# Causal attention: the probabilities of chunks 0 and 1 turned by the DMA in fp16 pairs, attended as one pair

## The reference, cut to what matters

```
energy = einsum('bhsk,bhtk->bhst', Q, K)          # 16 heads of 32 channels
lengths = sum(energy[:, :, 0, :] != 0, axis=-1)
energy = where(cols >= lengths, -inf, energy)
energy = where(cols[None, :] > cols[:, None], -inf, energy)
score = softmax(energy / sqrt(dk), axis=-1)
out = einsum('bhst,bhtk->bhsk', score, V) * m
x1 = layernorm(x + out)
```

## Time and profile before

| | us |
|---|---|
| median of 3 runs (lowest, highest) | 2641.38 (2639.04, 2642.63) |
| the profiled execution, its own time | 2641.75 |
| its span (first to last instruction) | 2640.0 |

### The profile page before, as it was taken

How to read it: one execution, slowest core, us unless ns; L and a number is a source line. 1 busy time by engine, 2 the same in 40 slices (tenths; PEclk the granted TensorE clock), 3 DMA queues, 4 the chain that set the end, 5 groups by cost and what they waited for, 6 DMA issues and landing times.

```text
span 2640.0 us, 67260 instructions
## 1 busy us (share of the span) xinstructions
PE 2585.4 (98%) x23144; PEld 2230.3 (84%) x23144; DVE 1940.1 (73%) x5443; ACT 1553.5 (59%) x4738; POOL 923.6 (35%) x1102
## 2 busy tenths in 40 slices
PE   6999999999999999999999999999999999999997
PEld 5888888887888888888888888888788888888886
DVE  7888898887433444345388888888788888888877
ACT  6778778785111111111287777777676776767764
POOL 5776677751101010101013333333333434334341
PEclk8999999999999999999999999999999999999999
DMA  6676677674211111203021111112322212222210
GB/s 190 162 189 172 174 171 179 174 181 136 64 48 55 41 51 44 63 32 106 21 82 48 48 48 48 48 48 81 117 73 71 88 64 74 85 65 98 68 48 25
DMA packets 313622, 236.12 MB, mean 89 GB/s; under 512 B 150736, under 2 KB 240848, under 8 KB 312656
## 3 DMA queue, kind: packets, MB, share of 16 engines
q1 hardware_dynamic: 313552, 235.22, 31.3%
HBM read 137.65 MB, written 63.96 MB: 76 GB/s over the span
## 4 chain that ended last, share of the span: by engine, by line
PE 75%; DVE 11%; ACT 8%; issue 5%; DMA 1%; POOL 0%; DVEq 0%; SPq 0%; ACTq 0%; POOLq 0%
PE cross_work L181 16%; PE mlp_f L3282 13%; PE mlp_acc L3300 13%; PE causal_work L181 10%; PE cross_scores L2298 3%; PE cross_scores L2275 2%; PE cross_attended L2328 2%; PE causal_scores L2298 2%; ACT mask_prob L975 2%; PE causal_scores L2275 2%; DVE mask_scores L1560 2%; PE mask_work L181 2%; ACT mask_prob_even L975 2%; PE causal_attended L2328 2%; DVE mask_stats L1473 1%
## 5 line engine op out<-in xcount | busy, mean ns | idle before, releaser
L3075 ACT ACTIVATE mlp_h<-mlp_f,mlp_b1col 128x512 f32<-128x512 f32 x128 | 88.3, 690 | 526.6 <-PE mlp_f L3282 526.6
L3282 PE MATMUL mlp_f<-mlp_xT_hi,mlp_w 128*128 128x512 f32 x1024 | 335.4, 389 | 0.0
L3182 DVE CAST mlp_hT_hi<-mlp_h 128x512 fp32r<-128x512 f32 x128 | 58.3, 455 | 369.8 <-ACT mlp_h L3075 369.6
L3300 PE MATMUL mlp_acc<-mlp_w,mlp_hT_hi 128*128 128x512 f32 x1024 | 315.2, 389 | 0.0
L975 ACT ACTIVATE cross_prob<-cross_scores,cross_low 128x256 f32<-128x256 f32 x512 | 237.5, 490 | 63.4 <-DVE cross_low L1554 63.4
L975 ACT ACTIVATE causal_prob<-causal_scores,causal_low 128x128 f32<-128x128 f32 (+1 forms) x512 | 210.6, 437 | 93.7 <-DVE causal_low L1560 93.6
L3282 PEld LDWEIGHTS mlp_f<-mlp_xT_hi,mlp_w 128*128 128x128 f32 x1024 | 192.1, 188 | 40.6 <-DVE mlp_xT_lo L3168 0.4
L3300 PEld LDWEIGHTS mlp_acc<-mlp_w,mlp_hT_hi 128*128 128x128 f32 x1024 | 192.2, 188 | 39.9
L1560 DVE CUSTOM_DVE_ANT_0 mask_scores<-mask_scores,mask_mask 128x256 f32<-128x256 f32 x512 | 200.5, 459 | 28.7 <-PE mask_scores L2275 24.2
L181 PE MATMUL causal_work<-causal_xT_hi,causal_w 128*128 128x256 f32 x1008 | 217.0, 293 | 0.3 <-DVE causal_qk_parts L1508 0.3
L736 POOL TENSOR_SCALAR causal_q<-all_own_head,causal_qk_parts 128x128 fp32r<-128x128 f32 x128 | 60.7, 486 | 405.9 <-DVE causal_qk_parts L1508 395.6
(11 more groups left out here) (370 smaller groups left out, 8072.4 us busy)
## 6 DMA issues: line engine op xcount, KB each, us to landing
cross_x_in<-after_attention SPq DMA_DIRECT2D x17, 512.0 KB, 4.0
mask_x_in<-in_x SPq DMA_DIRECT2D x16, 512.0 KB, 4.5
mask_c_in<-in_ctx SPq DMA_DIRECT2D x16, 512.0 KB, 4.8
mask_res<-in_x SPq DMA_DIRECT2D x16, 512.0 KB, 3.7
after_attention<-mask_res SPq DMA_DIRECT2D x16, 512.0 KB, 3.3
mlp_x<-after_attention SPq DMA_DIRECT2D x8, 1024.0 KB, 5.5
mlp_stage<-in_L_xattn_fc_w SPq DMA_DIRECT2D x8, 1024.0 KB, 5.7
after_layer<-mlp_y SPq DMA_DIRECT2D x8, 1024.0 KB, 4.4
```

What stands on the lines that cost most here:

```text
L3282: ins = pe.matmul(F1[m % 2][:], W[2 * (m // 4)][:, a, k, m % 4 * P:(m % 4 + 1) * P], xT[p][:, k, :], start=(k == 0 and n == 0), stop=(k == ...
L3300: ins = pe.matmul(ACC[t][:], hT[a][:, m % 2, t * P:(t + 1) * P], W[2 * (m // 4) + 1][:, p, m % 4, :], start=(m == 0 and n == 0), stop=(m = ...
```

## The change

In the turns 1 to 14 of the causal phase, chunks 0 and 1 go the way of the mask phase's even chunks. `exps` of them writes to a new buffer `prob_even` of four heads; ACT's `causal_high` writes their fp16 high halves to `P16` and POOL's `causal_low` the low halves, two heads a step; SP issues two transposing DMAs a chunk (`causal_over`) to `PT16`, which has room for both chunks; `causal_parts` attends both chunks, five products each, directly ahead of `scores(b, 3)`. The eight `turn_probs` and `copy` of these chunks go. V's even parts are split in three. The turn has programs of its own, `causal_loop`, on ACT, DVE, PE and a branch on POOL, and their order differs from `causal_turn` in more than that, as the diff shows. The counts of `copied` follow (`turned_before`); the cross phase waits for the last such attend before it loads over the new buffers. The lift by 10 is added to `low` as in the mask phase.

```diff
--- before.py
+++ after.py
...
@@ -297,6 +300,13 @@
     if causal:
+        low = r("low", [P, 4, TT, 2])
+        at_end = room(REST + 44 * KB, 27 * KB)
+        prob_even = at_end("prob_even", [P, 4, 3 * P])
+        P16 = at_end("prob_parts", [P, 2, 2, 2, 3 * P], F16)
+        PT16 = at_end("probT_parts", [P, 2, 2, 2, 2, 3, P], F16)
+        VP = [at_end(f"v_part{i}", [P, TT, 2, P], BF16) for i in range(3)]
+        V_EVEN = V[:, :, 0:2 * HC].rearrange("p t (g h) d -> p t g (h d)", g=2)
...
@@ -381,21 +391,27 @@
-    def crossed(c):
-        return masked_ctx and c % 2 == 0
+    def crossed(b, c):
+        return masked_ctx and c % 2 == 0 or causal and not isinstance(b, int) and 0 <= c < 2
     def turned_before(b, c):
-        return turned_by_pe(kind) * b + HC * (c // 2 if masked_ctx else c)
+        if masked_ctx:
+            return UNITS // 2 * b + HC * (c // 2)
+        if cross or isinstance(b, int) and b == 0:
+            return UNITS * b + HC * c
+        if not isinstance(b, int) or b < B - 1:
+            return UNITS // 2 * b + UNITS // 2 + HC * (c if c < 0 else max(0, c - 2))
+        return UNITS // 2 * (B - 1) + UNITS // 2 + UNITS * (b - B + 1) + HC * c
     def low_of(u, qt):
-        return low[:, u % 4, qt, 0:1] if masked_ctx else low[:, u % 4, qt:qt + 1]
+        return low[:, u % 4, qt:qt + 1] if cross else low[:, u % 4, qt, 0:1]
     def probs(b, c):
-        if crossed(c):
+        if masked_ctx and crossed(b, c):
...
@@ -492,6 +508,14 @@
             sp.dma_start(tokens(dst, b), (res if masked_ctx else y)[:]).then_inc(stored, IT)
+        def causal_over(b, c):
+            hold(sp, s["av_done"], KC * b - KC + c + 1, s)
+            for i in range(2):
+                hold(sp, s["p_low"], 8 * b + 4 * c + 2 * i + 2, s)
+                sp.dma_start_transpose(PT16[:, c, i].rearrange("p a u k s -> p (a u k) s"),
+                                       P16[:, i].rearrange("p a u n -> p (a u n)")).then_inc(s["probs_turned"], IT)
...
@@ -549,6 +573,7 @@
             sp.wait_ge(last["x_seen"], B)
+            sp.wait_ge(last["av_done"], KC * (B - 2) + 2)
...
@@ -580,6 +605,9 @@
                 normed_by_quads(b + 1)
+            over = causal and (not isinstance(b, int) or b == B - 2)
+            if over:
+                causal_over(b, 0)
...
@@ -686,6 +721,13 @@
+        def causal_low(b, c, i):
+            pool.wait_ge(s["p_high"], 4 * b - 4 + 2 * c + i + 1)
+            for u in range(2):
+                pool.tensor_tensor(P16[:, i, 1, u], prob_even[:, 2 * i + u], P16[:, i, 0, u], ALU.subtract
+                                   ).then_inc(s["p_low"], 1)
...
@@ -814,6 +856,20 @@
                 return
+            if causal and not isinstance(b, int):
+                query0(b, 1)
+                query0(b, 2)
+                causal_low(b, 0, 0)
+                causal_low(b, 0, 1)
+                query0(b, 3)
+                values_left(b)
+                causal_low(b, 1, 0)
+                causal_low(b, 1, 1)
+                values_low(b)
+                query0(b + 1, 0)
+                last_norm(b)
+                last_gain(b)
+                return
...
@@ -964,7 +1023,11 @@
             c, h = u // HC, u % HC
-            if crossed(c):
+            if causal and crossed(b, c):
+                act.wait_ge(s["lifted"], 8 * b - 8 + HC * c + h + 1)
+                if h == 0:
+                    act.wait_ge(s["p_low"], 8 * b + 4 * c)
+            elif crossed(b, c):
...
@@ -972,8 +1035,10 @@
                 w = WIDTH[qt]
-                ins = act.activation(probs(b, c)[:, u % 4, qt, 0:w], SC[h][:, FROM[qt]:FROM[qt] + w], ACT.Exp,
-                                     bias=lifted[:, u % 4, qt:qt + 1] if crossed(c) else low_of(u, qt), scale=-1.0,
+                to = (prob_even[:, h, FROM[qt]:FROM[qt] + w] if causal and crossed(b, c)
+                      else probs(b, c)[:, u % 4, qt, 0:w])
+                ins = act.activation(to, SC[h][:, FROM[qt]:FROM[qt] + w], ACT.Exp,
+                                     bias=lifted[:, u % 4, qt:qt + 1] if crossed(b, c) else low_of(u, qt), scale=-1.0,
...
@@ -982,9 +1047,16 @@
             if u % HC == 0 and (c >= 2 or not isinstance(b, int) or b > 0):
-                act.wait_ge(s["av_done"], KC * b + c - 1)
+                act.wait_ge(s["av_done"], KC * b + c - (3 if causal and not isinstance(b, int) else 1))
             n = sum(WIDTH)
             act.activation(probT[:, u % RING, 0:n], probs_bank(b, u)[:, 0:n], ACT.Copy).then_inc(s["copied"], 1)
+        def causal_high(b, c, i):
+            if i == 0:
+                act.wait_ge(s["probs_turned"], IT * (4 * b + 2 * c))
+            act.wait_ge(s["exp_done"], UNITS * b + HC * c + 2 * i + 2)
+            act.activation(P16[:, i, 0], prob_even[:, 2 * i:2 * i + 2], ACT.Copy).then_inc(s["p_high"], 1)
...
@@ -1122,6 +1194,51 @@
                 yield ROOM
+        def causal_loop(b):
+            copy(b, -1)
+            exps(b, 0)
+            attended(b, -2, 2)
+            values(b, 0)
+            exps(b, 1)
+            exps(b, 2)
+            exps(b, 3)
+            qk(b, 2)
+            causal_high(b, 0, 0)
+            causal_high(b, 0, 1)
+            exps(b, 4)
+            exps(b, 5)
+            exps(b, 6)
+            qk(b, 3)
+            exps(b, 7)
+            turned(b + 1, 0)
+            turned(b + 1, 1)
+            values_high(b)
+            causal_high(b, 1, 0)
+            causal_high(b, 1, 1)
+            exps(b, 8)
+            exps(b, 9)
+            values_middle(b)
+            qk(b + 1, 0)
+            exps(b, 10)
+            exps(b, 11)
+            copy(b, 8)
+            copy(b, 9)
+            copy(b, 10)
+            copy(b, 11)
+            attended(b, 0, 2)
+            exps(b, 12)
+            exps(b, 13)
+            exps(b, 14)
+            exps(b, 15)
+            copy(b, 12)
+            copy(b, 13)
+            copy(b, 14)
+            qk(b + 1, 1)
...
@@ -1531,9 +1650,9 @@
                 masks_and_minima(b, HC * c + h)
-                if crossed(c) and h > 0:
+                if crossed(b, c) and h > 0:
                     lift(b, c, h - 1)
-            if crossed(c):
+            if crossed(b, c):
...
@@ -1781,6 +1900,36 @@
                 chain.k += 2
+        def causal_loop(b):
+            minima(b, 0)
+            cuts(b, 1)
+            turn_over(b + 1, 0)
+            attended(b, -2, 2)
+            qk_lo(b, 2)
+            turn_over(b + 1, 1)
+            minima(b, 1)
+            cuts(b, 2)
+            values(b, 1)
+            qk_lo(b, 3)
+            turned(b + 1, 0)
+            turned(b + 1, 1)
+            minima(b, 2)
+            cuts(b, 3)
+            add_z(b)
+            rows_kept(b)
+            qk_lo(b + 1, 0)
+            minima(b, 3)
+            row_stats()
+            ln_var(b, 0)
+            rows_seen(b + 1)
+            attended(b, 0, 2)
+            cuts(b + 1, 0)
+            qk_lo(b + 1, 1)
...
@@ -2329,6 +2481,21 @@
                 ins.then_inc(s["av_done"], 1)
+        def causal_parts(b, c):
+            pe.wait_ge(s["probs_turned"], IT * (4 * b + 2 * c + 2))
+            if c == 0:
+                pe.wait_ge(s["v_low"], b)
+            at = S * c
+            for kt in range(TT):
+                for n, (a, v) in enumerate(PARTS16):
+                    for h in range(HC):
+                        ins = pe.matmul(O[h * DH:(h + 1) * DH, at + kt * P:at + S],
+                                        VP[v][:, kt, c, h * DH:(h + 1) * DH],
+                                        PT16[:, c, h // 2, a, h % 2, 2 * kt:2 + kt, :],
+                                        start=(kt == 0 and n == 0), stop=(kt == 1 and n == len(PARTS16) - 1))
+            ins.then_inc(s["av_done"], 1)
...
@@ -2545,6 +2712,53 @@
+        def causal_loop(b):
+            turn_probs(b, -1)
+            scores(b, 0)
+            attend(b, -2, 2)
+            pe.wait_ge(s["qk_lo"], KC * b + 2)
+            queries(b, 2)
+            attended(b, -2, 2)
+            energies0(b, 1)
+            keys(b, 2)
+            pe.wait_ge(s["v_ready"], 2 * b + 1)
+            values(b, 1, 0)
+            scores(b, 1)
+            pe.wait_ge(s["qk_lo"], KC * b + 3)
+            queries(b, 3)
+            values(b, 1, 1)
+            keys(b, 3)
+            energies0(b, 2)
+            scores(b, 2)
+            energies0(b, 3)
+            pe.wait_ge(s["t_lo"], NP * (b + 1) + 1)
+            pe.wait_ge(s["qk_lo"], KC * (b + 1))
+            queries(b + 1, 0, 0)
+            pe.wait_ge(s["t_lo"], NP * (b + 2))
+            queries(b + 1, 0, 1)
+            keys(b + 1, 0)
+            turn_probs(b, 8)
+            turn_probs(b, 9)
+            values(b + 1, 0, 0)
+            turn_probs(b, 10)
+            turn_probs(b, 11)
+            attend(b, 0, 2)
+            scores(b, 3)
+            pe.wait_ge(s["qk_lo"], KC * (b + 1) + 1)
+            queries(b + 1, 1)
+            attended(b, 0, 2)
+            keys(b + 1, 1, 0)
```

(6 more changed lines are left out.)

50 lines of the change are left out of this document (35 added, 15 removed).

## The result

The changed kernel takes 2756.3 us (median of 4 runs, 2753.0 to 2757.0); the kernel before, on the same chip, 2642.0 (2639.0 to 2643.0). The ratio is 1.0432, with an interval of 1.0414 to 1.0450: 114 us slower, or 8.2 us in each of the 14 turns of the causal loop.

The account below looks back on a forecast made before the run. PE's queue bounds the kernel before; after the change a ring across engines, A to F, of 40.8 us a turn against 32.7 does. 2641.4 + 114 + 7 for the clock = 2762 us, range 2670 to 2812.

Parts of the forecast that it names:

- a ring, not a queue: Causal loop: waits across engines close into a ring A to F of 40.8 us a turn, not PE's 30.3 us queue.
- A: From the start of minima(b, 3) on DVE to the next turn's energies0 on PE, via POOL's norm: 13.8 us.
- B: From energies0(b, 1) through DVE's cuts, attended and qk_lo, and POOL's query0, to chunk 0's four lows: 9.15 us.
- C: On ACT, behind chunk 0's lows because prob_even is one buffer: four exps and four copies, 5.35 us.
- D: On POOL: values_left, 1.2 us, ahead of chunk 1's four lows, 3.6 us; 4.8 us together.
- E: Issue and landing of the turn's last transposing DMA: 0.1 + 4.5 us.
- F: On PE: the attend, 1.7 us, and scores(b, 3) until minima(b, 3) starts, 1.4 us; 3.1 us together.
- The clock: PE's halved clock after waits, put on the attend and scores: 0.5 us a turn, 7 in all, bounds 0 and 2.8.
- the waits foreseen: PE waits each turn: 2 to 3 us at energies0(b, 1), 3 at scores(b, 2), 3 at the attend.
- Rival 3: Causal loop: PE's queue still sets the turn, 30.3 us, giving 2608 us; chance 0.06.
- Rival 2: Causal loop: lows and transposes are hidden and only step A bites, 0.9 us a turn: 2654 to 2696 us; chance 0.13.

Follow-up runs that it names:

- the filled one: The changed kernel with never-read matmuls of the weights added in PE's three waits, to keep its clock up: 2739.8 us, ratio 1.0381.
- experiment on the kernel before: The kernel before with only row_stats and ln_var moved behind minima(b, 3): 2716.9 us, ratio 1.0286.
- the turn of 38.75 us above: One turn without halved clock in the changed kernel with six head buffers in prob_even instead of four; that kernel took 2752.4 us, ratio 1.0420.
- the second reordered kernel: The changed kernel with six head buffers, row_stats and ln_var early, and a new order on PE, ACT and DVE, attend behind scores(b, 3): 2687.8 us, ratio 1.0181.
- the first: The changed kernel with row_stats and ln_var early, six head buffers, energies0(b, 3) behind queries(b + 1, 0), and two DVE qk_lo moved ahead: 2686.8 us, ratio 1.0173.
- the third: The first reordered kernel with its remaining waits taken one by one, by further moves on PE, DVE, ACT and POOL: 2686.0 us, ratio 1.0171.

## Why the prediction came out right, step by step

The time was forecast at 2762 us and is 2756; the sign, the place and the form (a ring, not a queue) were right. The closeness of the total flatters the sum: two groups of errors of 1.3 and 1.5 us a turn nearly cancel, and that is luck, as the steps show. They can be read in the changed kernel (turn of 40.97 us, from `minima(b, 3)` to the next) and in the filled one at full clock (39.55 us, M3 at 1586.82 and 1626.37):

| step | forecast | after | after, filled |
|---|---|---|---|
| A, M3 to `energies0(b, 1)` | 13.8 | 13.83 | 13.81 |
| B, to the last low of chunk 0 | 9.15 | 9.18 | 9.08 |
| C, to ACT's next start behind `values_high` | 5.35 | 5.25 | 5.26 |
| D, to the last low of chunk 1 | 4.8 | 5.79 | 5.18 |
| E, to the attend of chunk 1 (after: of chunk 0) | 4.6 | 3.76 | 3.88 |
| F, to M3 | 3.1 | 3.16 | 2.34 |
| sum | 40.8 | 40.97 | 39.55 |

For instance B in the changed kernel: 1728.21 to 1733.84 + 3.55. Or E there: lows end at 1703.39 + 4.07, PE attends at 1711.22.

- **A, B and C** were right to 0.1 us. Their prices were rows of the same or like instructions or, for the lows, a proportion between two bounds: 0.9 was forecast and 0.89 measured. The experiment on the kernel before confirms A by itself, 13.84 us.
- **D** was mis-sized by 0.4 at full clock. `values_left` (1.38 us in the filled kernel) and the hand-over cost 1.6 and not 1.2, and nothing was allowed for engines that slow each other.
- **E** was mis-sized by 0.7: I kept the landing of a transpose with 16 tiles, 4.5 us, for one with 12. It is 3.8, while in proportion to the tiles it would be 3.4. The 2.9 us by the Trainium skill ("DMA: Bandwidth & Descriptors", anatomy of one DMA) are an estimate that is further off, on the other side; that section fits DMAs issued by GpSimd, and these are transposes issued by SP.
- **F** failed as a step: 1.7 us for the attend behind the landing, where at full clock only chunk 1's half of it (0.94) is behind. Its price as a whole was right (1.76 us from the attend to `scores(b, 3)`).
- **The clock** was mis-sized: 0.5 us a turn forecast, 40.97 - 39.55 = 1.4 measured. PE reaches the attend so late that both its halves lie behind (0.8, in F), and POOL's work falls beside DVE's (0.6, in D; this goes with where the work comes to lie, since the turn of 38.75 us above has lows of 4.06 us at full clock). The two bounds I gave, 0 and 2.8, hold it, but the place was wrong: I put the cost on the attend and the scores behind it, and no halved stretch falls there in any turn. In the turn shown it ends at 1708.09, 3.1 us ahead of the attend.

So E and F erred by 1.5 us a turn on one side, D and the clock by 1.3 on the other. Of the waits foreseen, those at `energies0(b, 1)` (1.9, forecast 2 to 3) and `scores(b, 2)` (2.2, forecast 3) are there; the one of 3 us at the attend isn't, being hidden by PE's own lateness, which is also why taking it away gave 0.65 us. The one of 0.7 at `energies0(b, 3)` I hadn't foreseen.

PE's own work in a turn, where no clock is halved, is 30.6 us in the second reordered kernel (35.42 less 4.82 of waits), 30.7 in the first and 31.8 in the third; the forecast had 30.3. Rival 3 (2608) would have needed that and no waits. Rival 2 named step A alone; the experiment on the kernel before prices that step at 3.7 us a turn and 1.7 for the clock on top. The forecast of 0.9 us had PE's saving taken off first and nothing for the clock.

What is still open: how the remaining 3.3 us of a turn in the reordered kernels divide among DVE's and ACT's hand-overs.

## What to carry to other kernels

Before an operation is put behind another, follow what it releases in the other engines' queues: two small DVE calls, moved behind four minima, held POOL's norm back by 4.6 us, put it between PE and its next operand and cost 76 us by themselves. When work leaves the bounding engine, ask what it covered; eight transposes of 0.33 us were also time in which minima, exps and copies could come in. And add a ring up step by step from rows of the same shape: the sum was good because three of six steps had such rows, while each of the others was off by 0.4 to 0.8 us and the errors happened to cancel.
